# Attention: two heads per stack in the array's row halves, exponentials two banks wide, maxima issued in pairs, V kept in SBUF

## The chip, the cores and the metric

One of the eight cores of a Trainium2 chip runs the whole program. The metric is the device time of one execution in microseconds; the time before is the median of three runs.

## The reference, cut to what matters

Two layers; only the first attention is touched. Its weights and inputs are float32 (2 batches, 1024 tokens, 256 features, 16 heads).

```python
qkv = layernorm(x) @ W_attn                  # q1 k1 q2 k2 (128 columns each), v (256)
attn1 = q1 @ k1.T * hd**-0.5                 # per head, hd = 8
attn2 = q2 @ k2.T * hd**-0.5
score = softmax(attn1 - lam * attn2)         # 1024 x 1024 per head, 16 heads, 2 batches
x = x + ((1 - LAMBDA_INIT) * (score @ v)) @ W_proj
```

After it come a ternary feed-forward layer, a linear attention with 32 heads and a routed layer.

## The kernel before, in words

Instructions are placed by hand: each engine runs its own list in order and waits on semaphores. Six stages follow each other; between two of them all engines meet, and a stage may start only when every engine has reached its end.

`stage_qkv` (L157) normalizes x in four chunks of 512 tokens, transposes them and multiplies by W_attn. Every product is made of a rounded high part and the low rest, three matmuls each. With the scale and lambda folded into Q, one head is 16 rows of Q and 16 of K, and the score is one product. SyncE (L213 to L245) stores high and low parts of Q and K of each chunk to DRAM (L233) and then the chunk's V (four stores, L237), whose rows are padded to 32 columns a head, with a one in column 16. V waits for ScalarE's eviction (L366). After chunk 1 SyncE issues the loads of the first stack. The stage ends for SyncE when that stack has landed (L245). POOL (L248) fills the padding: two V buffers and, by `pad` (L430), the rows of two stacks that no load writes; VectorE meanwhile normalizes chunk 0 (L114, L123, L141) and scales the row of factors (L316, L317), for which TensorE waits at L385.

`stage_attention` (L440) works on groups of four heads, eight groups over both batches. A **stack** (`qst`, `kst`, three of each in turn) holds the four heads one behind the other: on 128 partitions, of which 50 carry data: Q high, Q low, Q high against K high, K high, K low, and two rows of minus the maximum (high and low) against ones. `load_stack` (L417) fills it with seven DMAs. For each group:

- **Maxima** (L572): 64 matmuls 128x512, queries on the partitions, go to three PSUM banks `ps_m` in turn; VectorE reduces each (L710). Then `finish_max` makes the row of 4096 maxima, and SyncE writes it into the stack with eight small DMAs (L535).
- **Scores** (L592): 64 matmuls 128x512, keys on the partitions, into three banks `ps_s`; the two extra rows subtract the maximum. ScalarE exponentiates each (L684) into `prob`.
- **Values** (L605): for every 128 keys and 512 queries one value unit, four heads side by side in four strips of 32 columns of the array, in float32 (two instructions a matmul), summed over the eight key tiles in one of two `ps_o` banks. The one in V's column 16 gives the sum of the exponentials.
- **Out**: ScalarE copies the bank (L691), TensorE transposes it (L578) through `ps_m`, VectorE divides (L720 to L723).

The order on TensorE is written out. Score units are numbered u; a unit is one head and 128 keys and has two score matmuls. `side` gives the maxima and transposes that stand beside unit u; the maxima of group g+1 start six units ahead of group g, two a unit; value units follow at u % 4 = 1 and 3:

```python
side[max(-1, UPG * (g - 1) - LEAD + m // MPU)].append(("max", g, m))
```

`side[-1]` holds what runs before the first score: all 64 maxima of group 0 and 12 of group 1. The ternary weights of the next stage are made beside them (ScalarE L660 to L675, POOL L546 to L554, transposes L631 between the maxima), in the memory of `prob`. `pe.wait_ge(m_rd, n - BANKS + 1)` lets maximum n start when the third before it is reduced; `pe.wait_ge(exp_ok, n - BANKS + 1)` does the same for scores.

Of the kernel before, what the change touches and what calls it, by code (L numbers as in the profile page):

```python
# [22 lines left out]
P = 128  # L23
# [133 lines left out]
def stage_qkv(nc, d, io, keep, scratch):  # L157


    with ExitStack() as ctx:  # L160
        st = Store(nc, ctx, "qkv")
        X, ident, qst = keep["X"], keep["ident"], keep["qst"]
        q_dram, v_dram, zero_dram = scratch["qk"], scratch["v"], scratch["zero"]
# [6 lines left out]
        qk_lo = st.sb("qk_lo", [P, 2, NQ, d.CH], F32R)  # L170

        v_st = [st.sb("v_st", [P, d.TPC, d.H, 32])[:],
                keep["tern"][:].rearrange("p a n -> p (a n)").bitcast(F32)
                .rearrange("p (t h c) -> p t h c", t=d.TPC, h=d.H)]
# [3 lines left out]
        VG = d.H // d.G  # L178

# [18 lines left out]
        qk_out, v_out = scratch["qk_out"], scratch["v_out"]  # L198
        v_ps, v_ok, v_init, pad_ok, z_out = (st.sem(n) for n in ("v_ps", "v_ok", "v_init", "pad_ok", "z_out"))
# [12 lines left out]
        with nc.Block() as block:  # L212
            @block.sync  # L213
            def _(sp):
# [10 lines left out]
                sp.wait_ge(pad_ok, 1)  # L225
                sp.dma_start(zero_dram, as_f32(qst[0][64:66]).rearrange("r h t -> r (h t)")).then_inc(z_out, 16)
                for c in range(d.NC):
# [7 lines left out]
                    sp.wait_ge(v_ok, 2 * (c + 1))  # L235
                    for g in range(VG):
                        sp.dma_start(v_dram[b, g, :, t0 // P:t0 // P + d.TPC, :],  # L237
                                     v_st[c % 2][:, :, d.G * g:d.G * (g + 1), :].rearrange("p t h c -> p t (h c)"))\
                            .then_inc(v_out[c % 2], 16)
                    if c == d.S // d.CH - 1:  # L240
                        sp.wait_ge(z_out, 16)
# [6 lines left out]
            def _(pool):  # L248
# [80 lines left out]
            def _(act):  # L329
# [17 lines left out]
                for c in range(d.NC):  # L347
# [12 lines left out]
                    for j in range(2):  # L360
                        act.wait_ge(v_ps, 2 * c + j + 1)
                        if c < 2:
                            act.wait_ge(v_init, c + 1)
                        else:
                            act.wait_ge(v_out[c % 2], 16 * VG * (c // 2))
                        nc.scalar.activation(v_st[c % 2][:, 2 * j:2 * j + 2, :, 0:d.HD],  # L366
# [47 lines left out]
STACK_LOADS = 7  # L414


def load_stack(d, keep, scratch, g, sp, sem):  # L417
# [3 lines left out]
    for base, dst, parts in ((0, qst, (0, 1, 0)), (d.E, kst, (0, 0, 1))):  # L421
        for n, part in enumerate(parts):
            src = scratch["qk"][part, b, base + h0 * d.HD:base + (h0 + d.G) * d.HD, :]
            sp.dma_start(as_f32(dst[n * d.HD:(n + 1) * d.HD, :, :]),
                         src.rearrange("(h e) t -> e h t", e=d.HD)).then_inc(sem, 16)
    sp.dma_start(as_f32(qst[3 * d.HD:3 * d.HD + 2, :, :]), scratch["zero"].rearrange("r (h t) -> r h t", h=d.G))\
        .then_inc(sem, 16)


def pad(nc, link, keep, i):  # L430

    qst, kst = keep["qst"][i], keep["kst"][i]
    link(nc.gpsimd.memset(as_f32(qst[64:P, :, :]), 0.0))
    link(nc.gpsimd.memset(as_f32(kst[64:P, :, :]), 0.0))
    link(nc.gpsimd.memset(as_f32(qst[32:64, :, :]), 0.0))
    return nc.gpsimd.memset(as_f32(kst[32:64, :, :]), 1.0)

# [1779 lines left out]
```

## Time and profile before

| what | us |
|---|---|
| median of three runs (lowest, highest) | 1344.59 (1342.28, 1345.54) |
| span of the profiled execution | 1344.7 |
| its TensorE, busy | 1139.2 (85%) |
| its VectorE, busy | 921.8 (69%) |
| its ScalarE, busy | 630.1 (47%) |
| its POOL, busy | 231.4 (17%) |
| mean granted clock of TensorE | 0.911 |

Busy time is the time in which an engine had at least one instruction in work, over the whole program. TensorE's matmuls overlap, so what one costs in a row of them is the distance between their starts, not its duration. "PEld" is TensorE's weight load, which runs beside the matmul before. A granted clock of 1.00 is 2.4 GHz, 0.50 is 1.2 GHz. "SPq" is SyncE's queue, which issues the DMAs. "Idle before" is the engine's idle time ahead of an instruction, with what ended it.

### The profile page before, as it was taken

The page shows a single profiled execution, that of the slowest core. Times are in us where ns is not written, and L with a number is a line of the kernel's source. Part 1 is how long each engine was busy: PE and PEld are TensorE (multiplying, and loading weights), DVE is VectorE, ACT ScalarE, POOL GpSimd, SP SyncE. Part 2 cuts the span into 40 slices and gives each one's busy share as a digit, 9 for nine tenths or more (in the row PEclk, how much of TensorE's full clock was granted, in tenths as well). Part 3 has the DMA queues.
Part 4 walks back from the last instruction along what each step waited for, and adds up shares of the span by engine and source line. Part 5 has one row for each costly group of instructions (what it writes and reads, how often), then busy time and mean ns, then how long its engine had stood idle before and what let it go on. Part 6 is the DMA issues. An engine that isn't in the chain of part 4 may idle for free. (4 is left out here: it accounts for less than half of the span.)

```text
span 1344.7 us, 16323 instructions
## 1 busy us (share of the span) xinstructions
PE 1139.2 (85%) x5920; PEld 820.3 (61%) x5920; DVE 921.8 (69%) x1953; ACT 630.1 (47%) x1106; POOL 231.4 (17%) x178
## 2 busy tenths in 40 slices
PE   0959999999999998655575747999999799999888
PEld 0834555555555533544464635888887589889786
DVE  8739888888888820458988867555554677777743
ACT  2413766676666676267664213333333433433233
POOL 9006300000000000100003322100000644744200
PEclk9965999999999999777787878999999899999859
DMA  2794422421431000000000020100000000000200
GB/s 87 213 287 66 65 33 34 64 41 26 64 39 28 1 2 32 4 1 0 1 1 1 1 82 1 48 17 32 33 16 0 32 1 1 1 1 1 83 0 4
DMA packets 34221, 48.55 MB, mean 36 GB/s; under 512 B 5310, under 2 KB 22218, under 8 KB 34122
## 3 DMA queue, kind: packets, MB, share of 16 engines
q1 hardware_dynamic: 34140, 47.51, 16.0%
q8 instruction: 47, 0.77, 0.2%
q14 instruction: 34, 0.28, 0.1%
HBM read 32.52 MB, written 14.71 MB: 35 GB/s over the span
## 5 line engine op out<-in xcount | busy, mean ns | idle before, releaser
L710 DVE TENSOR_REDUCE att_mx<-att_ps_m 128x1 f32<-128x512 f32 x512 | 316.3, 681 | 66.8 <-PE att_ps_m L572 66.8
L684 ACT ACTIVATE att_prob<-att_ps_s 128x512 f32<-128x512 f32 x512 | 267.2, 604 | 115.6 <-PE att_ps_s L592 115.5
L572 PE MATMUL att_ps_m<-kst,qst 128*128 128x512 f32 x512 | 227.5, 468 | 18.5 <-PEq L74 16.0
L592 PE MATMUL att_ps_s<-qst,kst 128*128 128x512 f32 x512 | 200.7, 404 | 4.9 <-ACT att_prob L684 4.7
L572 PEld LDWEIGHTS att_ps_m<-kst,qst 128*128 128x128 f32 x512 | 102.3, 200 | 142.2 <-DVE att_mx L710 111.0
L1719 POOL TENSOR_TENSOR qry_prod<-qry_qr,lin_ksum 128x512 f32<-128x512 f32 x64 | 87.9, 1375 | 307.3 <-ACT qry_qr L1786 307.3
L605 PE MATMUL att_ps_o<-att_prob,att_vst 128*32 128x512 f32 x1024 | 136.2, 604 | 0.0
L592 PEld LDWEIGHTS att_ps_s<-qst,kst 128*128 128x128 f32 x512 | 94.8, 188 | 42.3 <-ACT att_prob L684 27.8
L1786 ACT ACTIVATE qry_qr<-qry_ps_q 128x512 f32<-128x512 f32 x64 | 38.3, 598 | 129.8 <-PE qry_ps_q L152 116.4
L1462 DVE SCALAR_TENSOR_TENSOR key_k_lo<-key_ps_k,key_k_hi 128x512 fp32r<-128x512 f32 x64 | 44.2, 690 | 67.8 <-ACT key_k_hi L1542 67.3
L1103 ACT ACTIVATE mlp_junk<-mlp_z,mlp_nlev 128x1024 bf16<-128x1024 f32 x64 | 72.6, 1137 | 23.2 <-DVE mlp_nlev L939 21.6
L152 PE MATMUL qry_ps_o<-qry_m_hi,qry_n_hi 128*128 128x256 f32 x256 | 76.5, 299 | 0.9 <-DVE qry_n_lo L1749 0.8
L152 PE MATMUL qry_ps_o<-qry_m_lo,qry_n_hi 128*128 128x256 f32 x256 | 71.0, 277 | 0.0
L152 PE MATMUL qry_ps_o<-qry_m_hi,qry_n_lo 128*128 128x256 f32 x256 | 70.9, 277 | 0.0
L1749 DVE TENSOR_TENSOR qry_n_lo<-qry_ps_t,qry_n_hi 128x512 fp32r<-128x512 f32 x64 | 44.2, 691 | 37.3 <-ACT qry_n_hi L1775 36.9
L1542 ACT ACTIVATE key_k_hi<-key_ps_k 128x512 fp32r<-128x512 f32 x64 | 38.2, 597 | 66.0 <-PE key_ps_k L152 65.3
L829 POOL CAST mlp_wo_t<-ternary 128x2048 f32<-128x2048 bf16 x1 | 1.9, 1891 | 386.4 <-POOLq L508 386.4
L152 PE MATMUL key_ps_k<-key_w_hi,lin_xt_hi 128*128 128x512 f32 x128 | 54.2, 424 | 1.7 <-DVE lin_xt_lo L1421 1.7
L1739 DVE SCALAR_TENSOR_TENSOR qry_qn<-qry_rec,qry_qr 128x512 f32<-128x512 f32 x64 | 53.5, 836 | 2.2
L152 PE MATMUL qry_ps_q<-qry_w_hi,lin_xt_hi 128*128 128x512 f32 x128 | 51.7, 404 | 3.3 <-DVE qry_w_lo L1759 3.3
L152 PE MATMUL qry_ps_q<-qry_w_lo,lin_xt_hi 128*128 128x512 f32 x128 | 51.5, 402 | 0.0
L152 PE MATMUL key_ps_g<-key_k_hi,key_xk_hi 128*128 128x512 f32 x128 | 50.5, 395 | 0.6 <-DVE key_k_lo L1462 0.6
(348 smaller groups left out, 2395.6 us busy)
## 6 DMA issues: line engine op xcount, KB each, us to landing
qst<-qk_parts SPq DMA_DIRECT2D x24, 256.0 KB
kst<-qk_parts SPq DMA_DIRECT2D x24, 256.0 KB
qk_parts<-att_out SPq DMA_DIRECT2D x16, 256.0 KB, 3.3
qk_parts<-qkv_qk_lo SPq DMA_DIRECT2D x16, 256.0 KB, 3.4
att_vst<-v_rows SPq DMA_DIRECT2D x8, 512.0 KB
residual<-L_attn_x SPq DMA_DIRECT2D x4, 512.0 KB, 5.7
v_rows<-qkv_v_st SPq DMA_DIRECT2D x8, 256.0 KB, 5.4
v_rows<-ternary SPq DMA_DIRECT2D x8, 256.0 KB, 4.0
```

Of the source, the lines that this page charges most:

```text
L152: ins = nc.tensor.matmul(out, a, b, start=first and n == 0, stop=last and n == len(terms) - 1)
L572: nc.tensor.matmul(ps_m[:, n % BANKS, :], qst[g % RING][:, h, t * P:(t + 1) * P], kst[g % RING][:, h, half * d.CH:(half + 1) * d.CH], star ...
L592: nc.tensor.matmul(ps_s[:, n % BANKS, :], kst[g % RING][:, h, s * P:(s + 1) * P], qst[g % RING][:, h, t * d.CH:(t + 1) * d.CH], start=True ...
L605: ins = nc.tensor.matmul(ps_o[32 * h:32 * h + 32, t, :], vst[g % RING][:, s, 32 * h:32 * h + 32], prob[:, n % RING, h, t * d.CH:(t + 1) * ...
L684: nc.scalar.activation(prob[:, s % RING, h, t * d.CH:(t + 1) * d.CH], ps_s[:, n % BANKS, :], ACT.Exp).then_inc(exp_ok, 1)
L710: nc.vector.reduce_max(mx[:, g % 2, m // NB, m % NB:m % NB + 1], ps_m[:, n % BANKS, :], AX.X)\
L1103: nc.scalar.activation(junk[:, n % 2, :], Z[:, t, :], ACT.Sign, bias=nlev[:, t:t + 1], accum_out=sgn[:, t:t + 1]).then_inc(cnt_ok, 1)
L1462: nc.vector.scalar_tensor_tensor(out=k_lo[:, i % 2, :], in0=ps_k[:, i % 2, :], scalar=0.0, in1=as_f32(k_hi[:, i % 2, :]), op0=ALU.max, op1 ...
L1719: nc.gpsimd.tensor_tensor(prod[:, u % 2, :], qr[:, u % 2, :], ksum[:, b, cols(n)], ALU.mult).then_inc(pr_ok, 1)
L1739: nc.vector.scalar_tensor_tensor(out=qn[:, u % 2, :].rearrange("p (h e) -> p h e", e=HW), in0=rec[:].unsqueeze(2).to_broadcast([P, HPB, HW ...
L1749: nc.vector.tensor_tensor(n_lo[:, u % 2, :], ps_t[:, u % 2, :], as_f32(n_hi[:, u % 2, :]), ALU.subtract).then_inc(n_ok, 1)
L1786: nc.scalar.activation(qr[:, u % 2, :], ps_q[:, u % 2, :], ACT.Relu).then_inc(q_ok, 1)
```

## The change

A stack now has two heads above each other: rows 0 to 49 hold heads 0 and 2 of the group, rows 64 to 113 (`ROW2` = 64) heads 1 and 3, one pair behind the other. Matmuls take 48 or 50 rows of one half, so two of them (a pair) address the two halves of the array's rows and write two banks. Score pairs have two times two banks, and one exponential reads two banks (1024 columns). Max pairs use three banks `ps_m`, maxima stay 512 columns each. `ps_o` is one bank. A step u is now 128 keys, 512 queries and four heads: two score pairs, two max pairs, and the value work of an earlier step (`LAG`), cut in two halves of 256 queries, except for the first key tile. The order of loops becomes group, query half, key tile. V stays in SBUF (`vall`), so its stores and loads and the zero rows go. A stack is loaded with 12 DMAs, a row of maxima written with 16. POOL fills `vall` and 32 rows of each half of `kst`; nothing is filled in the attention stage.

```diff
@@ stage_qkv: SyncE @@
-                sp.wait_ge(pad_ok, 1)
-                sp.dma_start(zero_dram, as_f32(qst[0][64:66]).rearrange("r h t -> r (h t)")).then_inc(z_out, 16)
...
-                    sp.wait_ge(v_ok, 2 * (c + 1))
-                    for g in range(VG):
-                        sp.dma_start(v_dram[b, g, :, t0 // P:t0 // P + d.TPC, :],
...
@@ stage_qkv: POOL @@
-                for i in range(2):
-                    link(nc.gpsimd.memset(v_st[i], 0.0))
-                    nc.gpsimd.memset(v_st[i][:, :, :, d.HD:d.HD + 1], 1.0).then_inc(v_init, 1)
-                    pool.wait_ge(v_init, i + 1)
-                for i in range(len(qst) - 1):
-                    pad(nc, link, keep, i).then_inc(pad_ok, 1)
+                link(nc.gpsimd.memset(vall[:], 0.0))
+                nc.gpsimd.memset(vall[:, :, :, d.HD:d.HD + 1], 1.0).then_inc(v_init, 1)
+                pool.wait_ge(v_init, 1)
+                for i in range(2 * len(kst)):
+                    rows = slice(ROW2 * (i % 2) + 32, ROW2 * (i % 2) + 64)
+                    nc.gpsimd.memset(as_f32(kst[i // 2][rows, :, :]), 1.0).then_inc(pad_ok, 1)
                     pool.wait_ge(pad_ok, i + 1)
@@ load_stack @@
-            sp.dma_start(as_f32(dst[n * d.HD:(n + 1) * d.HD, :, :]),
-                         src.rearrange("(h e) t -> e h t", e=d.HD)).then_inc(sem, 16)
...
+            for r in range(2):
+                row = ROW2 * r + n * d.HD
+                sp.dma_start(as_f32(dst[row:row + d.HD, :, :]), src[r]).then_inc(sem, 16)
@@ stage_attention: sizes and order @@
-        LEAD = 6
-        SUM_AT, TURN_AT = 34, (64, 71)
+        PR = 6
+        LEAD = 5
+        LAG = 2
+        HALF = d.CH // 2
+        SUM_AT, TURN_AT = 17, (32, 37)
...
+        SPG = NS * NB
+        MPG = PAIRS * NS * NB
+        STEPS = SPG * d.NG
+        NMD = 16
...
+                side[max(-1, SPG * (g - 1) - LEAD + m // PAIRS)].append(("max", g, m))
             for t in range(NB):
+                side[NS * (NB * g + t + 1) + LAG + 2].append(("out", g, t))
...
+        for u in range(STEPS):
+            for c in range(2):
+                slot = 2 * (u + LAG) + c
+                if u % NS < 2:
+                    slot = 2 * (u // NS * NS + LAG + 1) + u % NS
+                values.setdefault(slot, []).append((u, c))
@@ stage_attention: TensorE @@
                     if kind == "max":
+                        if n + 1 >= MB:
+                            pe.wait_ge(m_rd, n + 2 - MB)
...
+                        for r in range(2):
+                            rows = slice(ROW2 * r, ROW2 * r + 3 * HD)
+                            ins = nc.tensor.matmul(ps_m[:, (n + r) % MB, :], qst[g % RING][rows, j, t * P:(t + 1) * P],
+                                                   kst[g % RING][rows, j, half * d.CH:(half + 1) * d.CH],
+                                                   start=True, stop=True)
+                        ins.then_inc(m_ps, 2)
...
+                def score_pair(u, j):
...
+                        pe.wait_ge(exp_ok, p - 1)
+                    for r in range(2):
+                        rows = slice(ROW2 * r, ROW2 * r + 3 * HD + 2)
+                        ins = nc.tensor.matmul(ps_s[:, 2 * (p % 2) + r, :], kst[g % RING][rows, j, s * P:(s + 1) * P],
+                                               qst[g % RING][rows, j, t * d.CH:(t + 1) * d.CH], start=True, stop=True)
+                    ins.then_inc(sc_ps, 1)
+
+                def value_half(u, c):
...
+                    cols = slice(c * HALF, (c + 1) * HALF) if s else slice(0, d.CH)
                     for h in range(G):
+                        ins = nc.tensor.matmul(ps_o[32 * h:32 * h + 32, cols], vall[:, NS * b + s, h0 + h, :],
+                                               prob[:, u % PR, h, cols], start=s == 0,
+                                               stop=s == NS - 1 and c == 1)
...
+                for u in range(END):
                     todo = side[u]
+                    for j in range(PAIRS):
+                        if u < STEPS:
+                            score_pair(u, j)
                         for x in todo[:1]:
                             side_unit(*x)
                         todo = todo[1:]
+                        for v in values.get(2 * u + j, []):
+                            value_half(*v)
                     for x in todo:
                         side_unit(*x)
@@ stage_attention: ScalarE @@
+                        nc.scalar.activation(prob[:, u % PR, 2 * j:2 * j + 2, :],
+                                             ps_s[:, 2 * (p % 2):2 * (p % 2) + 2, :], ACT.Exp).then_inc(exp_ok, 1)
@@ stage_attention: VectorE @@
+                        dve.wait_ge(m_ps, n + 2)
+                        for r in range(2):
+                            nc.vector.reduce_max(mx[:, g % 2, r, m:m + 1], ps_m[:, (n + r) % MB, :], AX.X)\
+                                .then_inc(m_rd, 1)
```

## Rows read from the trace of the kernel before

**Rows 1.** The stages' windows: us, busy us (instructions) by engine, PEclk, DMA share, GB/s

```profile
0.00:89.70 89.70, 41.13 (x226) 35.95 (x227) 56.32 (x115) 25.92 (x46) 32.92 (x19) 0.93 0.64 186
89.70:139.00 49.30, 46.54 (x112) 25.05 (x112) 48.34 (x80) 16.58 (x18) 27.51 (x9) 0.60 0.51 108
139.00:477.50 338.50, 337.77 (x1776) 175.24 (x1776) 284.09 (x498) 233.15 (x449) 7.14 (x3) 1.00 0.29 39
477.50:531.00 53.50, 48.80 (x262) 17.69 (x259) 2.83 (x12) 41.41 (x80) 0.00 (x0) 1.00 0.01 1
531.00:1344.70 813.70, 664.99 (x3552) 566.39 (x3550) 530.26 (x1251) 313.03 (x514) 163.79 (x149) 0.88 0.05 16
```

**Rows 2.** Waits of 139 to 477 us: waited for, us in total, times, longest

```profile
ACT att_prob L684 <- PE att_ps_s L592: 105.2, 112, 1.4
```

**Rows 3.** Timeline of one period of the main part: start, us, engine, line

```profile
172.30 0.39 PE L572 MATMUL att_ps_m<-kst,qst 128*128 128x512 f32 x1
...
172.53 0.39 PE L592 MATMUL att_ps_s<-qst,kst 128*128 128x512 f32 x1
...
172.84 0.16 PEld L605 LDWEIGHTS att_ps_o<-att_prob,att_vst 128*32 128x32 f32 x8 [0.35 <-ACT att_prob L684]
172.84 1.06 PE L605 MATMUL att_ps_o<-att_prob,att_vst 128*32 128x512 f32 x8
...
173.84 0.50 PE L572 MATMUL att_ps_m<-kst,qst 128*128 128x512 f32 x1
...
174.18 0.39 PE L592 MATMUL att_ps_s<-qst,kst 128*128 128x512 f32 x1
...
174.38 2.48 DVE L710 TENSOR_REDUCE att_mx<-att_ps_m 128x1 f32<-128x512 f32 x4 [0.55 <-PE att_ps_m L572]
```

**Rows 4.** Timeline of the first 36 us: VectorE, POOL, TensorE

```profile
5.78 3.51 POOL L433 MEMSET qst<- 64x4096 f32 x1
...
6.73 2.58 DVE L114 TENSOR_SCALAR qkv_ve<-qkv_mv 128x4 f32<-128x4 f32 x1
...
13.11 14.24 DVE L141 TENSOR_SCALAR qkv_xn<-residual,qkv_mv,qkv_rstd 128x256 f32<-128x256 f32 x4
...
32.41 2.00 DVE L316 TENSOR_SCALAR qkv_row<-qkv_row,qkv_lam 1x64 f32<-1x64 f32 x1
...
34.49 0.58 PE L385 MATMUL qkv_ps_v<-qkv_one,qkv_row 1*128 1x1 f32 x2 [5.06 <-DVE qkv_row L317]
```

**Rows 5.** Timeline around the gap before attention

```profile
67.22 12.30 SPq L237 DMA_DIRECT2D v_rows<-qkv_v_st  x4
...
73.72 0.60 ACT L366 ACTIVATE ternary<-qkv_ps_v 128x512 f32<-128x512 f32 x1 [0.83 <-PE qkv_ps_v L152]
...
85.66 3.19 SPq L237 DMA_DIRECT2D v_rows<-ternary  x4
...
89.69 0.93 PEld L572 LDWEIGHTS att_ps_m<-kst,qst 128*128 128x128 f32 x3 [16.21 <-issue]
```

**Rows 6.** One window inside that gap

```profile
76.00:78.00 2.00, 0.00 (x0) 0.00 (x0) 0.00 (x0) 0.00 (x0) 0.00 (x0) 0.94 1.06 394
```

**Rows 7.** Timeline of attention's opening

```profile
90.52 38.39 DVE L710 TENSOR_REDUCE att_mx<-att_ps_m 128x1 f32<-128x512 f32 x64 [18.35 <-PE att_ps_m L572]
...
91.27 0.29 PEld L572 LDWEIGHTS att_ps_m<-kst,qst 128*128 128x128 f32 x1 [0.65 <-DVE att_mx L710]
...
132.25 2.52 SPq L535 DMA_DIRECT2D qst<-att_nm_hi  x4
```

**Rows 8.** Groups of instructions, shapes apart: busy us, mean ns, idle before

```profile
L684 ACT ACTIVATE att_prob<-att_ps_s 128x512 f32<-128x512 f32 x512 | 267.2, 604 | 115.6 <-PE att_ps_s L592 115.5
...
L660 ACT ACTIVATE att_prob<-att_prob 128x2048 f32<-128x2048 f32 x2 | 3.8, 1911 | 27.7 <-DMA att_prob<-L_ffn_W_syn 25.3 <-DMA att_prob<-L_ffn_W_out 2.4
...
L2123 PE MATMUL rt_ps_a<-rt_h,rt_gate 128*8 128x256 f32 x32 | 7.4, 379 | 0.0
...
L605 PE MATMUL att_ps_o<-att_prob,att_vst 128*32 128x512 f32 x1024 | 136.2, 604 | 0.0
```

More of the change, by code:

```diff
@@ L446, in stage_attention @@
         st = Store(nc, ctx, "att")
-        AO, ident, qst, kst, tern, sc = (keep[n] for n in ("AO", "ident", "qst", "kst", "tern", "sc"))
+        AO, ident, qst, kst, tern, sc, vall = (keep[n] for n in ("AO", "ident", "qst", "kst", "tern", "sc", "v"))
         NS = d.S // P
@@ L483, in stage_attention, with place @@
         TB = d.KT * d.N // d.CH
-        UPG = NS * G
-        MPG = G * NS * NB
-        MPU = MPG // UPG
-        UN = UPG * d.NG
-        LOADS = STACK_LOADS + 1
-        NMD = 8
-        side = {u: [] for u in range(-1, UN + 2 * G + 3)}
+        SPG = NS * NB
+        MPG = PAIRS * NS * NB
+        STEPS = SPG * d.NG
+        NMD = 16
+        END = STEPS + LAG + 4
+        side = {u: [] for u in range(-1, END)}
         for g in range(d.NG):
             for m in range(MPG):
-                side[max(-1, UPG * (g - 1) - LEAD + m // MPU)].append(("max", g, m))
+                side[max(-1, SPG * (g - 1) - LEAD + m // PAIRS)].append(("max", g, m))
             for t in range(NB):
-                side[UPG * (g + 1) + G + 2 + t].append(("out", g, t))
-        items = [(u, x) for u in side for x in side[u]]
+                side[NS * (NB * g + t + 1) + LAG + 2].append(("out", g, t))
+        items = [x for u in side for x in side[u]]
+        first, total = {}, 0
+        for x in items:
+            first[x] = total
+            total += 2 if x[0] == "max" else 1
+        values = {}
+        for u in range(STEPS):
[4 more added lines that the diff above has]
+                values.setdefault(slot, []).append((u, c))
         def loaded(g):
-            return 16 * (LOADS * (g // RING + 1) - (STACK_LOADS if g % RING == 0 else 0))
-        def ready(kind, g, m):
-            return [x for _, x in items].index((kind, g, m)) + 1
+            return 16 * STACK_LOADS * (g // RING + (0 if g % RING == 0 else 1))
+        def place(kind, g, m):
+            return first[kind, g, m] + 1
         with nc.Block() as block:
@@ L556, in _ @@
                     pool.wait_ge(tern_ok, i + 1)
-                pad(nc, link, keep, RING - 1).then_inc(pad_ok, 1)
             @block.tensor
             def _(pe):
-                done = [0]
                 def side_unit(kind, g, m):
-                    n = done[0]
-                    done[0] += 1
-                    if n >= BANKS:
-                        pe.wait_ge(m_rd, n - BANKS + 1)
+                    n = first[kind, g, m]
                     if kind == "max":
-                        h, t, half = m // (NS * NB), m // NB % NS, m % NB
+                        if n + 1 >= MB:
+                            pe.wait_ge(m_rd, n + 2 - MB)
+                        j, t, half = m // (NS * NB), m // NB % NS, m % NB
@@ L570, in side_unit @@
                         if m == 0 and g:
                             pe.wait_ge(load[g % RING], loaded(g))
-                        nc.tensor.matmul(ps_m[:, n % BANKS, :], qst[g % RING][:, h, t * P:(t + 1) * P],
-                                         kst[g % RING][:, h, half * d.CH:(half + 1) * d.CH],
-                                         start=True, stop=True).then_inc(m_ps, 1)
+                        for r in range(2):
[3 more added lines that the diff above has]
+                                                   start=True, stop=True)
@@ L638, in _ @@
                         prologue[TURN_AT[i] + k] = lambda i=i, k=k: turn_weight(i, k)
-                for n, x in enumerate(side.pop(-1)):
+                for n, x in enumerate(side[-1]):
                     side_unit(*x)
```

174 lines of the change are left out of this document (70 added, 104 removed).

## The prediction

> **What bounds the kernel now.** I read the windows by stage first: the scaled input projection and everything ahead of the attention stage take 89.7 us, the attention stage's opening (maxima of the first head group alone, weights made ternary) 49.3, its main part 338.5, its tail without maxima 53.5, and the rest of the program 813.7, which the change does not touch [rows 1]. In the main part TensorE is busy throughout, at full granted clock; VectorE 84%, ScalarE 69%. The waits there say the same: ScalarE waits 105.2 us of it for scores [rows 2]. One period of the timeline shows why TensorE binds: matmuls of 512 columns follow each other every 0.23 us, eight of them (four maxima, four scores), then 0.08 us to get into the value unit, 1.00 us for its eight instructions, and about 0.11 us to get out, which is 3.03 us; VectorE's four maxima fill 2.48 of it [rows 3]. 338.5 us hold 109 such periods (436 maxima), so 3.10 each with the transposes.
>
> **The front: POOL's fills.** POOL and VectorE share something here: L114's 4-element tensor_scalar, asked for at 6.73, lasts until 9.31, just behind POOL's fill of 5.78 to 9.29; the four L141 last 14.24 us, one fill each; L316 waits until 34.4 for the last fill; TensorE's L385 starts at 34.49 [rows 4]. The change replaces eight fills of 4096 elements per partition (3.51 each) and two of 2048 by one of 8192 (7.0), a small one (0.2 to 0.4) and six of 2048 on 32 partitions (half of 3.51, 1.76, plus 0.06 between). So POOL is done at about 20 instead of 34.4. VectorE: L114 ends with the large fill at 8.6, L123, three short steps later, with the first of the six at 10.8, the four L141 with a fill each: 12.6, 14.4, 16.3, 18.1, where they ended at 27.35. Gain so far 9.2. L316 came 5.1 after them, now at 23.2, when POOL is idle, and with L317 takes some 0.3 instead of 2.0: L385 at 23.5. **Gain 11.0**; bounds 9 (L316's part lost) and 12.
>
> **The gap before attention.** The last projection result leaves ScalarE at 74.3 and the first weight load of a maximum starts at 89.69. Between them SyncE is stuck in stores of V: the third chunk's four issues take 12.30 us from 67.22, the fourth's end at 88.85 [rows 5], and at 76 to 78 the DMA engines are still full, at 394 GB/s [rows 6]. With V kept in SBUF all 16 stores and 8 loads of V go, the stores of chunk 3's Q and K are issued as they are computed, and the stack (same bytes in 12 issues instead of 7, plus some 2 us of SyncE, hidden) should land by then, since it was issued ahead of all that. The stage then ends with ScalarE at 74.3 plus the 0.84 that 88.85 to 89.69 shows: 75.2. **Gain 14.4**; bounds 9 (the queue still holds SyncE up for 5 us) and 15.
>
> **The opening: costlier.** Here VectorE is the bound now, 64 maxima in 38.39 us, 0.60 each, with three banks [rows 7]. The change issues them in pairs into the same three banks, so that a pair may start only when one maximum of the pair before is left. VectorE frees a bank 0.75 us after it starts a maximum (90.52 to 91.27), and from a weight load to the maximum behind it takes 0.83 at the clock granted here (89.69 to 90.52; the clock falls during TensorE's pause, its mean is 0.94 at 76 to 78 and 0.60 over the opening [rows 1, 6]). If the two halves run side by side, a pair repeats every 0.75 + 0.83 + 0.01 = 1.59 us, not 1.20. 42 pairs (32 of group 0, 10 of group 1) stand before the first score; I take the last eight at full clock (1.28, below), since the transposes of the ternary weights stand between them and fill TensorE: 0.8 + 34 x 1.59 + 8 x 1.28 = 65 us instead of 49.3. The row of maxima goes out in 16 DMAs instead of 8, each 0.63 of SyncE [rows 7]: 10 us where 5 were; they start at about 53 of the 65 us and land at 64, just hidden. **Loss 15.8**. The ternary work runs beside it.
>
> **The main part.** I call half a step a slot: a score pair, a max pair, half a value unit. TensorE: weight load 0.11 (0.34 after a value unit less 0.23), two pair streams 0.46, 0.09 into value mode, the half unit. That form is in no row: it costs between 0.50 and 1.00. float32 instructions of 256 and 512 columns last 379 and 604 ns [rows 8], 0.225 apart, and two stand behind each other, so 1.00 - 0.45 = 0.55 to 0.57. I take 0.57: slot 1.23. VectorE: 0.75 until the bank is free, 0.54 from weight load to maximum at full clock (173.84 to 174.38): 1.28 per pair against 1.20 of work. ScalarE: 512 columns 0.604, 2048 columns 1.91 [rows 8], so 0.85 ns a column; 1024 take about 1.04, or 0.95 repeating. So VectorE, slowed by its three banks, sets the slot at 1.28. Eight steps (16 slots) are a round: 14 intervals of 1.28; one of 1.65, where TensorE has the undivided first value unit between two max pairs (0.11 + 0.23 + 0.09 + 1.00 + 0.22); and one of 3.3, with two value halves together (1.1), two score pairs (0.67), a max pair (0.23), four transposes (0.7) and another half (0.6). Sum 22.9 a round, against 8 x 3.10 = 24.8. 214 pairs are left, 13.4 rounds: 306 us instead of 338.5. **Gain 32.5**. The maxima's DMAs (2.7 us until issue, 9.5 of issues, 1.8 landing) have about 17 us here, so they stay covered.
>
> **The tail.** 21 steps have no maxima: a slot is 0.11 + 0.23 + 0.09 + 0.57 = 1.00 on TensorE, 0.95 on ScalarE; with the undivided units and transposes 17.5 a round, 46 in all, and 3.5 to finish, against 53.5. **Gain 4.**
>
> **Sum:** 1344.7 - 11.0 - 14.4 + 15.8 - 32.5 - 4.0 = 1298.6. The profiled execution spans 1344.7 us, the median of the runs is 1344.59, so nothing is to be corrected: 1299.
>
> **The pair's price.** Two halves of the rows at once stand in no row; the nearest is the value unit, where eight matmuls of 0.6 us in four column strips take 1.00 us together [rows 3]. A pair costs between one stream (0.23) and two (0.46). I take the first, by that row. The Trainium skill's TensorE: Matmul & The Clock Gate, section Part 3: Packing small matmuls, gives 3.07 times for four row tiles where four would be ideal; by that share a pair would be 0.30, 0.07 more, and my sum about 1322. No row here shows it.
>
> **Rivals.**
> *Weight loads queue.* If the two halves' weight loads follow each other (0.11 each; double at half clock), every pair is late by one: 34 x 0.21 + 8 x 0.11 + 214 x 0.11 + 42 x 0.11 = 36 us more: 1334. Against it: the value unit's eight loads take 0.16 us together. With partial overlap of the streams this case covers 1315 to 1340. Chance 0.18.
> *Slower: the halves run one after the other.* Pairs take 0.46: TensorE's slot is 0.11 + 0.92 + 0.09 + 0.57 = 1.69, and TensorE binds. Against the forecast: 34 x 0.43 + 8 x 0.23 in the opening (16), 0.41 x 14 + 1.1 a round (92), 0.23 x 42 in the tail (10): 1417. It decides from about 0.1 us of extra time per pair, some two fifths of a stream. Nothing in the trace excludes it; the strips speak against. Chance 0.10.
> *The clock.* TensorE would stream 0.89 of each 1.42 us, less than before, and in the opening much less. The tail (66% streaming, clock 1.00 [rows 1]) speaks against a fall in the main part. At clock 0.50 a slot is about 2.15 and a round 38.5; three such rounds of 13.4 undo the gain. Chance 0.06, two thirds of it slower. The other way: the shorter pause (1.7 us) leaves the clock up in the opening: pairs of 1.28, 10.5 us less, 1288. Chance 0.10.
> *Nothing gained inside attention* (PE's issue or semaphores fill what pairing frees), only front and gap: about 1335 to 1345. Chance 0.04, half of it no change.
>
> **Numbers.** The forecast has 0.52. Range 1280 (clock up in the opening, tail 5 better) to 1340. Within 0.3% (4 us, about what a measurement of this kernel can tell from no change) is 0.03, slower 0.14, faster 0.83.
>
> **What would show it.** L385 near 24 and the first maximum at about 64; the maximum's repeat 1.6 us per pair in the opening, 1.28 later; first score at about 129 and last maximum at about 435; VectorE waiting some 0.08 us per pair for TensorE. Wrong if row halves start 0.2 us apart, if granted clock falls after 130, or if scores wait for qst's maxima DMAs.

## The result and the profile after

The changed kernel takes 1327.5 us (median of 4 runs, 1320.2 to 1329.9) against 1343.7 (4 runs, 1342.3 to 1345.5): ratio 0.9862, interval 0.9831 to 0.9893. It is 16 us faster where 45 were forecast. The profiled execution took 1327.15 us and spans 1325.3, 26.7 more than the forecast sum of 1298.6. Of all the runs below one is left out of its median, g3's of 1323.6 us, which ran at a mean clock of 0.894 where g3's other three have 0.91 to 0.92. The windows below are the stages as the prediction cut them [rows 1]: projection, opening, main part, tail, rest of the program; columns as there.

```profile
0.00:63.60 63.60, 40.21 (x226) 35.21 (x227) 45.70 (x115) 25.90 (x46) 19.11 (x15) 1.00 0.58 171
63.60:130.60 67.00, 41.18 (x118) 18.10 (x118) 53.53 (x86) 16.52 (x18) 20.54 (x7) 0.51 0.39 95
130.60:455.60 325.00, 298.19 (x2472) 116.84 (x2474) 291.14 (x490) 224.22 (x229) 0.00 (x0) 0.93 0.21 29
455.60:514.00 58.40, 52.36 (x458) 18.51 (x450) 3.38 (x13) 42.64 (x45) 0.00 (x0) 0.85 0.01 2
514.00:1325.30 811.30, 666.44 (x3548) 567.22 (x3548) 529.85 (x1249) 312.79 (x514) 163.74 (x149) 0.89 0.05 16
```

Look at the granted clock: 0.93 in the main part and 0.85 in the tail, where before it was 1.00 in both. The opening is at 0.51, half clock throughout.

**Front and gap.** The timeline of the first 25 us, and what answers to [rows 4] in it; the last line, from the timeline of the weight loads, answers to [rows 5]:

```profile
1.53 6.92 POOL L243 MEMSET v_rows<- 128x8192 f32 x1
6.79 1.69 DVE L114 TENSOR_SCALAR qkv_ve<-qkv_mv 128x4 f32<-128x4 f32 x1
9.10 11.22 POOL L248 MEMSET kst<- 32x2048 f32 x6
11.16 7.42 DVE L141 TENSOR_SCALAR qkv_xn<-residual,qkv_mv,qkv_rstd 128x256 f32<-128x256 f32 x4
24.03 0.58 PE L372 MATMUL qkv_ps_v<-qkv_one,qkv_row 1*128 1x1 f32 x2 [3.37 <-DVE qkv_row L305]
...
63.60 0.21 PEld L558 LDWEIGHTS att_ps_m<-kst,qst 48*128 48x128 f32 x2 [1.50 <-issue]
```

VectorE's short instruction still ends with POOL's large fill (8.48 and 8.45), and the four L141 take 7.42 us instead of 14.24, beside POOL's shorter fills. POOL is done at 20.3, TensorE goes on at 24.03 instead of 34.49. The first maximum is at 63.60 instead of 89.69: 10.5 us of that are the front's, 15.6 the gap's.

**A full-clock slot.** The timeline of the main part around 262 us:

```profile
262.17 0.39 PE L582 MATMUL att_ps_s<-qst,kst 50*128 50x512 f32 x2
263.11 0.19 PEld L558 LDWEIGHTS att_ps_m<-kst,qst 48*128 48x128 f32 x2 [0.98 <-DVE att_mx L705]
263.12 0.49 PE L558 MATMUL att_ps_m<-kst,qst 48*128 48x512 f32 x2 [0.56 <-DVE att_mx L705]
...
264.40 0.50 PE L558 MATMUL att_ps_m<-kst,qst 48*128 48x512 f32 x2 [0.56 <-DVE att_mx L705]
```

The two matmuls of a pair stand in one row (x2): together they last 0.50 us, no more than one of them did before (0.39 to 0.50 [rows 3]). So the halves run side by side. What a pair costs in a row of them is the distance between starts; no pairs stand back to back here, but they do in f5 (below), whose filling pairs go to two banks and therefore have a row for each half:

```profile
76.37 0.39 PE L639 MATMUL att_ps_o<-kst,qst 48*128 48x512 f32 x1
76.37 0.39 PE L639 MATMUL att_ps_s<-kst,qst 48*128 48x512 f32 x1
76.60 0.39 PE L639 MATMUL att_ps_o<-kst,qst 48*128 48x512 f32 x1
76.61 0.39 PE L639 MATMUL att_ps_s<-kst,qst 48*128 48x512 f32 x1
```

A pair every 0.23 us is one stream's price. From one max pair to the next in the changed kernel it is 264.40 - 263.12 = 1.28 us, set by VectorE with three banks; TensorE idles 0.56 of it ahead of each of these two max pairs, because no value unit stands there. These two neighbouring idle pieces come once a round, and a single one of 0.55 us some 8 us behind them.

**The rounds.** Here is the main part cut at ScalarE's copies of the value bank (L683), one every eight steps, so that each window holds 32 maxima and the same matmuls (x188 of PE in each):

```profile
164.60:188.10 23.50, 21.35 (x188) 8.54 (x188) 22.22 (x40) 16.70 (x19) 0.00 (x0) 1.00 0.35 48
188.10:211.00 22.90, 21.07 (x188) 8.46 (x188) 21.39 (x36) 16.62 (x19) 0.00 (x0) 1.00 0.18 23
211.00:241.00 30.00, 28.17 (x188) 9.74 (x188) 22.14 (x40) 16.60 (x18) 0.00 (x0) 0.72 0.36 49
241.00:264.00 23.00, 21.03 (x188) 8.46 (x188) 21.49 (x36) 16.72 (x19) 0.00 (x0) 1.00 0.06 9
264.00:287.40 23.40, 21.34 (x188) 8.54 (x188) 22.12 (x40) 16.63 (x19) 0.00 (x0) 1.00 0.35 49
287.40:310.30 22.90, 21.07 (x188) 8.46 (x188) 21.39 (x36) 16.61 (x18) 0.00 (x0) 1.00 0.18 23
310.30:334.80 24.50, 22.56 (x188) 8.72 (x188) 22.22 (x40) 16.73 (x19) 0.00 (x0) 0.93 0.33 47
334.80:357.70 22.90, 21.08 (x188) 8.47 (x188) 21.39 (x36) 16.60 (x18) 0.00 (x0) 1.00 0.19 23
357.70:382.20 24.50, 22.62 (x188) 8.76 (x188) 22.15 (x40) 16.63 (x18) 0.00 (x0) 0.93 0.33 46
382.20:408.20 26.00, 24.13 (x188) 9.33 (x188) 21.45 (x36) 16.66 (x18) 0.00 (x0) 0.87 0.16 20
408.20:431.60 23.40, 21.32 (x188) 8.54 (x188) 22.12 (x40) 16.64 (x18) 0.00 (x0) 1.00 0.02 3
431.60:454.60 23.00, 21.06 (x188) 8.46 (x188) 21.49 (x36) 16.70 (x19) 0.00 (x0) 1.00 0.00 1
```

This table holds most of the answer. A round at full clock takes 22.9 us, as forecast, or 23.4 when VectorE also gathers a group's maxima (x40 of VectorE instead of x36). The four rounds with the clock below 1.00 (five falls, two of them in the round of 30.0) took 6.6, 1.1, 1.1 and 3.1 more than their like: 11.9 us. DMA shows no such link: at 0.35 one round took 23.4.

### The profile page after: what moved, and what is told of

The parts are those of the page before. It is cut to its first block and busy times, and to the rows that moved or that the text cites. A ratio compares the mean times of both kernels' runs of the same rounds, so it can differ in the third digit from the quotient of the medians.

```text
span 1325.3 us, 18000 instructions
## 1 busy us (share of the span) xinstructions
PE 1098.4 (83%) x6816; PEld 755.9 (57%) x6816; DVE 923.6 (70%) x1953; ACT 622.1 (47%) x850; POOL 203.4 (15%) x170
## 5 line engine op out<-in xcount | busy, mean ns | idle before, releaser
L705 DVE TENSOR_REDUCE att_mx<-att_ps_m 128x1 f32<-128x512 f32 x512 | 329.3, 685 | 37.5 <-PE att_ps_m L558 37.2
L675 ACT ACTIVATE att_prob<-att_ps_s 128x1024 f32<-128x1024 f32 x256 | 259.6, 1025 | 114.4 <-PE att_ps_s L582 114.0
L558 PE MATMUL att_ps_m<-kst,qst 48*128 48x512 f32 x512 | 135.7, 526 | 53.0 <-DVE att_mx L705 51.7
L598 PE MATMUL att_ps_o<-att_prob,v_rows 128*32 128x256 f32 (+1 forms) x1920 | 169.0, 434 | 2.6 <-ACT att_osb L683 2.6
L582 PE MATMUL att_ps_s<-qst,kst 50*128 50x512 f32 x512 | 131.4, 510 | 3.6 <-DMA qst<-att_nm_lo 2.1
L558 PEld LDWEIGHTS att_ps_m<-kst,qst 48*128 48x128 f32 x512 | 54.4, 209 | 112.5 <-DVE att_mx L705 98.1
L582 PEld LDWEIGHTS att_ps_s<-qst,kst 50*128 50x128 f32 x512 | 50.9, 196 | 107.8 <-issue 72.0
L598 PEld LDWEIGHTS att_ps_o<-att_prob,v_rows 128*32 128x32 f32 x1920 | 41.2, 112 | 68.6 <-issue 61.7
```

Source lines behind the costliest of these rows:

```text
L558: ins = nc.tensor.matmul(ps_m[:, (n + r) % MB, :], qst[g % RING][rows, j, t * P:(t + 1) * P], kst[g % RING][rows, j, half * d.CH:(half + 1 ...
L582: ins = nc.tensor.matmul(ps_s[:, 2 * (p % 2) + r, :], kst[g % RING][rows, j, s * P:(s + 1) * P], qst[g % RING][rows, j, t * d.CH:(t + 1) * ...
L598: ins = nc.tensor.matmul(ps_o[32 * h:32 * h + 32, cols], vall[:, NS * b + s, h0 + h, :], prob[:, u % PR, h, cols], start=s == 0, stop=s == ...
L675: nc.scalar.activation(prob[:, u % PR, 2 * j:2 * j + 2, :], ps_s[:, 2 * (p % 2):2 * (p % 2) + 2, :], ACT.Exp).then_inc(exp_ok, 1)
L705: nc.vector.reduce_max(mx[:, g % 2, r, m:m + 1], ps_m[:, (n + r) % MB, :], AX.X)\
```

## The experiments

Two theories. **Clock**: what is missing is TensorE at half clock. **Rival**: it is stalls that would be there at any clock (the maxima's transfers, the gathering of a group, banks), and the falls of the clock cost little. All kernels start from the changed one; "profile" is the span of the profiled execution.

### Filling TensorE's idle time in the opening

```
for n, x in enumerate(side[-1]):
    side_unit(*x)
+   for k in range(6):                     # rows 0.. into ps_o, rows 64.. into ps_s[3]; three, all into ps_o, from the 32nd pair on
+       nc.tensor.matmul(<bank>, qst[0][rows, 0, 0:P], kst[0][rows, 0, 0:d.CH], start=True, stop=True)
```

> The changed kernel with idle time of TensorE in the opening filled: behind each pair of maxima of the first group, six more matmuls of the same shape go into banks that nobody reads. Clock theory (the missing gain is TensorE at half clock): the granted clock comes back to 1.00 soon after the first maxima, a pair repeats every 1.28 us instead of 1.59, the opening lasts 54 to 57 us instead of 67.0, the first 17 us of the main part run at full clock too and give 3 more, so about 1311 to 1315 against the 1327.5 of the changed kernel. Rival (the pair repeat is set by VectorE and the three banks whatever the clock is): the opening stays at 67 and the time at 1327, or grows with the fillers to 1340. The main part after 30 us of it and the tail stay as they are under both.

1326.3 us (1325.3 to 1328.8), no gain. Yet the first part did what the clock theory says; two windows, and the timeline where they meet:

```profile
64.40:107.00 42.60, 39.67 (x261) 22.71 (x262) 41.76 (x67) 11.68 (x9) 18.64 (x7) 1.00 0.53 146
107.00:133.90 26.90, 24.48 (x76) 15.48 (x77) 13.81 (x21) 4.94 (x9) 2.04 (x1) 0.52 0.45 60
```

```profile
99.82 9.22 POOL L543 TENSOR_TENSOR att_prob<-att_prob 128x2048 f32<-128x2048 f32 x2
...
106.84 2.24 DVE L704 CAST att_nm_hi<-att_nmt 128x32 fp32r<-128x32 f32 x1
...
109.96 0.80 PE L559 MATMUL att_ps_m<-kst,qst 48*128 48x512 f32 x2 [2.42 <-DVE att_mx L713]
```

At full clock the pair repeats in 1.28 us and VectorE is 98% busy. Then VectorE's small copy, 0.18 us in other groups, lasts 2.24, to the end of POOL's subtraction; TensorE stands 2.42 us, and after that the matmul is at half clock (0.80 us). The fillers behind it, now slower (the 26.9 us window has clock 0.52), gave the gain back. So the opening has a second bound, POOL's work on the ternary weights.

### Filling the empty slots of the main part, and its control

Per eight steps two slots have no value unit. e2 issues the score pair twice there; f6 issues the same number of extra pairs in a step with two value halves. The two idle pieces stand half a slot later than the two doubled pairs, so in e2 only the first of them gets shorter:

```profile
258.24 0.50 PE L559 MATMUL att_ps_m<-kst,qst 48*128 48x512 f32 x2 [0.33 <-DVE att_mx L707]
...
259.53 0.50 PE L559 MATMUL att_ps_m<-kst,qst 48*128 48x512 f32 x2 [0.56 <-DVE att_mx L707]
```

Where this document and the expectations speak of filled slots, this is what was filled: 0.55 and 0.55 us became 0.33 and 0.56.

```
-for r in range(2):
+for k in range(2 if 2 * u + j in values else 4):      # f6: 4 if u % NS == 5 else 2
+    r = k % 2
     rows = slice(ROW2 * r, ROW2 * r + 3 * HD + 2)
     ins = nc.tensor.matmul(ps_s[:, 2 * (p % 2) + r, :], ...)
```

> The changed kernel with each score pair issued twice in the slots that have no value unit (two per eight steps, where TensorE idles 0.55 us twice, just ahead of most falls of the clock). Clock theory: these dips bring the granted clock down; filled, the falls in the main part (at 213, 223, 313, 360 and 382 us) are gone or fewer, which gives back up to 13 us of the main part: 1314 to 1320. Rival (the falls follow the maxima's last steps of a group, or come by chance): as many falls as before, 1327, and 0.2 us more per dip at worst, 1331.

> Control of e2: the same number of extra score pairs, two per eight steps, but in the step with two half value units, not in the empty slots. If what brings the clock down is the quiet stretch around the empty slots: the falls of the main part stay as in the changed kernel, and the extra pairs cost about 0.2 us each: 1330 to 1335. If it is TensorE's mean activity: the falls go as they did in e2, 1314 to 1320.

e2: 1316.3 us (1312.8 to 1329.5), ratio 0.9819 (0.9764 to 0.9874). The windows of its opening, main part and tail:

```profile
64.00:131.10 67.10, 41.19 (x118) 18.14 (x118) 53.53 (x86) 16.51 (x18) 20.56 (x7) 0.52 0.38 101
131.10:446.90 315.80, 293.03 (x2536) 122.01 (x2538) 291.07 (x490) 224.37 (x229) 0.00 (x0) 0.97 0.19 30
446.90:499.90 53.00, 47.90 (x462) 17.66 (x461) 3.45 (x14) 42.66 (x45) 0.00 (x0) 0.97 0.01 2
```

TensorE does more (x2536 for x2472), and main part and tail are 9 and 5 us shorter; against the second profiled execution of the changed kernel (f8 below: 321.3 and 57.9) it is 5.5 and 5. By the medians e2 gains 7 to 11 us (1323.6 and 1327.5 are the changed kernel's two medians). f6: 1323.0 (1319.3 to 1325.1), between its two expectations and no gain over the 1323.6 that the changed kernel took on the same chip; its profile has two falls in the main part where the changed kernel's has five.

What the profiles add, and what the expectations did not single out, is where the falls begin. In the five with these slots untouched and `LEAD` 5 (changed, f8, e1, f7, e4), 22 of the 23 falls in the rounds of the main part begin within 0.9 us behind the second of the two neighbouring idle pieces, and both of f6's do; the other, at 222.3 us of the changed kernel, follows the single piece by 1.8 us. In f6 TensorE's idle time in the rounds sums to 20.6 us, in e2 to 21.1, in the changed kernel to 23.2. So the sum of idle time doesn't tell e2 from f6; the neighbouring pieces do, which f6 leaves as they were. One profiled execution of each is little to go by, though, and e2's slowest run (1329.5, mean clock 0.885 where its profiled one had 0.900) shows that the falls become rarer, not impossible.

### The maxima one step further ahead

`LEAD = 6` instead of 5; g4 is that with e2's doubled scores.

> The changed kernel with the maxima one step further ahead of their scores (LEAD 6 instead of 5). At 466.4 us the first score of the last group waits 2.06 us for the maxima's transfers and the clock falls just behind it. If that wait is what brings the tail down to half clock: the wait is gone, the tail stays at 1.00 and lasts 50 us or less instead of 57.6; the opening gets two pairs longer (3.2 us) and the main part shorter by as much: about 1320. If the tail falls by itself, because it has no maxima and TensorE does less: the wait is gone, the fall stays, 1325 to 1327.

> LEAD 6 as in e3, with the doubled score pairs of e2. e3 was 10 us slower than the changed kernel, and its rounds of eight steps took 22.95 to 27.96 us with the clock falling once in most of them. If the falls are the whole of that: filled, the rounds are 23.1 to 23.7, main part and opening together 382 to 385 (e2: 382.2), and the time is that of e2, 1311 to 1317. If LEAD 6 has a cost of its own (a wait for a stack or for the maxima's buffers): rounds stay above 24 at full clock, 1325 to 1335.

e3: 1337.3 (1331.7 to 1339.3), 10 us slower, which neither side expected. The wait for the maxima's transfers ahead of the last group is gone, and still the tail has clock 0.91 (0.85 before) and lasts 56.7 us: that wait was not all that brings it down. The main part fell to 0.90. Its timeline shows why: the gathering of a group now comes right ahead of the empty slots, and TensorE idles 1.41 us in one piece where the longest in the changed kernel's rounds is 0.56; one max pair later it runs at half clock (0.80). Six such pieces of 1.40 us stand in its main part, and behind each the clock falls within 2.4 us.

```profile
215.90 0.39 PE L582 MATMUL att_ps_s<-qst,kst 50*128 50x512 f32 x2
217.70 0.64 PE L558 MATMUL att_ps_m<-kst,qst 48*128 48x512 f32 x2 [1.41 <-DVE att_mx L705]
...
219.12 0.80 PE L558 MATMUL att_ps_m<-kst,qst 48*128 48x512 f32 x2 [0.36 <-DVE att_mx L705]
```

g4: 1327.3 (1324.2 to 1329.2), a miss for the number: the doubled scores leave 1.01 us of that idle time, and its clock in the window of the table below is 0.95. Its undisturbed rounds take 23.1, as in e2, so LEAD 6 has no cost of its own at full clock.

### The stores of V put back

```
+sp.wait_ge(v_ok, 2 * (c + 1))
+for g in range(VG):
+    sp.dma_start(v_dram[b, g, :, t0 // P:t0 // P + d.TPC, :], <vall of chunk c>).then_inc(v_out[c % 2], 16)
# and, in the attention stage, SyncE waits for v_out ahead of the weights' loads
```

> The changed kernel with the 16 stores of V to DRAM put back in SyncE's queue of the projection stage, which nobody reads any more. If the gap ahead of attention (15.6 us of the gain measured) was SyncE held up by these stores: the first maximum starts at 76 to 79 us instead of 63.6 and the time is about 1340 to 1343. If it was something else that the change took away (the zero rows, the seventh load, the V loads behind them): the first maximum stays below 68 and the time at 1327 to 1331.

1337.3 us (2 runs), 3 below the expectation. SyncE's issues and the first maximum's weight load:

```profile
59.34 8.23 SPq L231 DMA_DIRECT2D v_spill<-v_rows  x3
...
77.67 0.32 PEld L565 LDWEIGHTS att_ps_m<-kst,qst 48*128 48x128 f32 x2 [15.15 <-issue]
```

The first maximum moves from 63.6 to 77.7, by 14.1 of the gap's 15.6 us: the gap was, all but 1.5 us, these stores in SyncE's queue. The time rose by less, 9.7 us against 1327.5 and 13.7 against the 1323.6 of f8, because main part and tail took 321.3 and 57.9 us, as in f8.

### A fourth bank for the opening's maxima

```
-ps_m = st.ps("ps_m", [P, MB, d.CH]);      ps_o = st.ps("ps_o", [P, d.CH])
+ps_m = st.ps("ps_m", [P, MB + 1, d.CH]);  ps_o = ps_m[:, MB, :]
+# maxima ahead of the first score: bank n % 4, wait for m_rd >= n - 2; behind it n % 3 as before
```

> The changed kernel with a fourth bank for the maxima of the opening (the value bank, not needed there yet). The prediction read the opening's pair as 0.75 until VectorE frees a bank plus 0.83 until the next maximum starts at half clock, because pairs share three banks. By that a pair repeats in VectorE's own 1.20 to 1.23 us although TensorE stays at half clock, the first group's maxima are done some 11 us earlier, and the opening is 56 to 62 us instead of 67.0 (ternary weights and the maxima's transfers become the bound): 1316 to 1322. Rival (half clock itself makes TensorE too slow for VectorE): the repeat stays near 1.6 and the time at 1327.

1308.6 us (1306.7 to 1312.2), ratio 0.9723 (0.9698 to 0.9748). Weight loads in its opening, and those of the changed kernel below:

```profile
75.12 0.29 PEld L565 LDWEIGHTS att_ps_m<-kst,qst 48*128 48x128 f32 x2 [0.90 <-DVE att_mx L712]
76.31 0.29 PEld L565 LDWEIGHTS att_ps_m<-kst,qst 48*128 48x128 f32 x2 [0.91 <-DVE att_mx L712]
77.51 0.29 PEld L565 LDWEIGHTS att_ps_m<-kst,qst 48*128 48x128 f32 x2 [0.91 <-DVE att_mx L712]
```

```profile
75.71 0.29 PEld L558 LDWEIGHTS att_ps_m<-kst,qst 48*128 48x128 f32 x2 [1.29 <-DVE att_mx L705]
77.29 0.29 PEld L558 LDWEIGHTS att_ps_m<-kst,qst 48*128 48x128 f32 x2 [1.30 <-DVE att_mx L705]
```

Both are at half clock (0.29 us a load); the repeat is 1.20 with four banks and 1.58 with three. The opening is 55.7 us instead of 67.0; that is 11.3 of the 14.9 us by which its profiled execution is shorter (1310.4). The main part gives 5.7 more (319.3 us at clock 0.95, for 325.0 at 0.93), the tail 0.6, and what follows attention was 2.7 longer. So the mechanism gives the 11, and it went below the 1316 expected by fewer falls of the clock, as the changed kernel itself does in its better runs. The forecast's reading of the opening, banks times half clock, holds to 0.01 us.

### The changed kernel again, and combinations

> The changed kernel as it is, for the spread of its runs against their mean granted clock. Clock theory: its runs differ by where the clock falls, so time and mean clock go together, about 0.4 us of time per us spent at half clock. Rival (the spread has another cause): times of 1320 to 1330 at the same mean clock.

1323.6 us median (1315.1 to 1324.3). The nine runs of the changed kernel span mean clocks from 0.880 (1329.9 us) to 0.893 (1315.1). With 2 x (1 - clock) x span as the time at half clock, these two are at 318.7 and 281.1 us: 14.8 us of time for 37.6 of half clock, 0.39 each, and a straight line through all nine gives the same 0.39 (correlation 0.99). The spread of the runs goes with the clock's. The five falls in the rounds of the changed kernel's profile give the same price: 11.9 us lost in 30.7 at half clock.

f5 has both fillers, the weights' sum five pairs earlier and the weight transposes two later; g1 the four banks, e2's doubled scores and the sum two pairs earlier; g2 is g1 with the scores three times; g3 is g1 with fillers in the opening and at its two waits, and the weight transposes two pairs later.

> The changed kernel with both fillers, the scores issued twice in the slots without a value unit and six filling matmuls behind each pair of the opening (while a score bank is free for them), and with the weights' sum put behind the 13th pair of maxima instead of the 18th and the weight transposes behind the 35th instead of the 33rd, so that POOL is done before VectorE gathers the first group's maxima (in e1 POOL's subtraction stretched VectorE's copy from 0.18 to 2.24 us, TensorE stood 2.4 us, and the clock fell). Clock theory: opening 55 to 60 us instead of 67.0, no half clock at the start of the main part (3 more), main part 312, tail 53 as in e2: 1311.0 of e2's profiled run less 10 to 14, about 1299 to 1304 for a run like it. Rival (something else holds the opening: the maxima's transfers or the ternary work): opening 64 to 67, 1308 to 1316.

> The four banks of the opening (f7) together with the doubled score pairs in the empty slots (e2), and the weights' sum behind the 16th pair instead of the 18th, as late as the weights themselves allow. If the two gains are what the traces say, they add: f7's profiled 1310.4, less some 5 to 6 for the falls in its main part, less 4 to 5 for the half clock in its tail, less 2 for POOL being done earlier: about 1298 to 1301. If the doubled pairs only moved the falls about by chance (e2's slowest run took 1329.5 us): 1306 to 1310.

> As g1, but the scores of the empty slots issued three times instead of twice, which fills 0.46 of the 0.55 us of idle time. Clock theory: as fast as g1 or up to 3 us slower in its profiled run, with less spread between its runs, since no run falls in the main part; rival (the score's delay of 0.46 us reaches ScalarE or VectorE): rounds of 23.6 us and more instead of 23.14, 3 to 8 us slower than g1 in all runs.

> As g1 with four filling matmuls behind each pair of the opening into two score banks, and sixteen of them at each of two waits (VectorE gathering the first maxima, the transfers of the maxima ahead of the first score), so that the clock is at 1.00 when the scores start. Clock theory: no half clock in the first 16 us of the main part, 3 us less than g1, 1295 to 1298. Rival (the fillers themselves hold up what follows, by up to 3.7 us each): 1300 to 1304.

The main part from the first copy of the value bank to the last maximum, the same work in each but for the extra pairs (and one pair of maxima or two less in e3 and g4), by the windows view:

| kernel | median us (runs) | profile, us | this window, us | granted clock |
|---|---|---|---|---|
| changed | 1327.5 (4) | 1325.3 | 290.3 | 0.95 |
| f8, changed again | 1323.6 (5) | 1321.8 | 286.8 | 0.96 |
| e1 | 1326.3 (4) | 1324.2 | 285.6 | 0.97 |
| f7, four banks | 1308.6 (4) | 1310.4 | 285.7 | 0.97 |
| e2, empty slots filled | 1316.3 (4) | 1311.0 | 280.6 | 1.00 |
| f5 | 1315.4 (4) | 1308.2 | 280.7 | 1.00 |
| g1, f7 with e2 | 1305.3 (6) | 1303.4 | 280.7 | 1.00 |
| g3 | 1304.7 (3) | 1302.8 | 280.6 | 1.00 |
| g2, scores three times | 1310.7 (5) | 1308.8 | 289.0 | 0.98 |
| f6, control | 1323.0 (4) | 1319.9 | 284.5 | 0.98 |
| e3, LEAD 6 | 1337.3 (6) | 1334.8 | 299.8 | 0.91 |
| g4, LEAD 6 with e2 | 1327.3 (4) | 1326.5 | 290.8 | 0.95 |
| e4, V's stores back | 1337.3 (2) | 1336.4 | 286.7 | 0.96 |

The four kernels with doubled scores and `LEAD` 5 are at 1.00 and within 0.1 us of each other; none of the seven without reached 1.00, and of the six with extra score pairs in the empty slots g2 and g4 did not either. **f5** missed its 1299 to 1304: the sum now came before the weights were there, TensorE waited for them at 81 us, and the clock fell there and again at 113 us, where its fillers had stopped and TensorE idled 0.94 and 0.79 us (opening 63.0 us). **g1**, at 1305.3 us (1301.1 to 1312.2), ratio 0.9701 (0.9676 to 0.9727), is 18 to 22 us below the changed kernel. g3, at 1304.7 (1302.8 to 1311.6), can't be told from it, and the lead of both over f7 is smaller than their spread. g1 missed its 1298 to 1301 mostly by the tail (56.6 us, e2's 53.0), which fell to half clock again:

```profile
64.20:118.90 54.70, 39.87 (x118) 17.89 (x119) 50.84 (x86) 16.55 (x18) 20.56 (x7) 0.52 0.40 119
118.90:434.20 315.30, 292.50 (x2534) 121.68 (x2536) 291.20 (x490) 224.11 (x229) 0.00 (x0) 0.97 0.21 31
434.20:490.80 56.60, 51.75 (x462) 18.83 (x462) 3.51 (x14) 42.76 (x45) 0.00 (x0) 0.88 0.01 2
```

**g2** idles 0.09 us, not 0.33, in the first of the two pieces, but 0.56 still in the second. Its other rounds are 0.24 us longer than g1's, and it has one long fall (28.9 us for that round, clock 0.76), which its clock theory excluded: more filling was no better. **g3** did bring the main part to 1.00 from the start (311.3 us, 4.0 less than g1), but its opening grew by 4.2 with the fillers, so its rival was right: the fillers cost what they give.

## Why the forecast was wrong

The direction was right and the time lies in the range, but the gain is a third of the forecast. By the prediction's steps, in us against its own numbers (what follows attention took 812 us, 2 less than before):

- **Front**, forecast -11.0: -10.5, by the mechanism named. VectorE's instructions end with POOL's fills, and L385 came at 24.03 for "near 24".
- **Gap**, -14.4: -15.6; shown by e4.
- **Opening**, +15.8: +17.7. The pair's 1.59 was 1.58, shown by f7 to be three banks times half clock. The first 34 pairs took 54.0 us, 0.9 less than forecast. Off was that the last eight run at full clock because the transposes fill TensorE: the clock stayed at half, and from 117.62 to the first score at 130.66 they took 1.63 each for 1.28, 2.8 us more. Where a group of transposes stands between two pairs TensorE has no idle time and the pairs are 1.77 apart, so there half clock makes TensorE the bound. The maxima's DMAs were hidden, as forecast: the 16 issues end at 125.3.
- **Main part**, -32.5: -13.6 (324.9 us for 306). The slot (1.28) and the round (22.9) are right. Of the 18.9 missing, 11.9 are the falls of the clock in four rounds, 3.4 the gathering of a group's maxima (0.5 in each of seven groups, left out of the sum), and the remaining 3.6 lie ahead of the first full round, where the clock was at half until 147 us. g3 supports this last part: with the clock up there it gained 4.0 over g1.
- **Tail**, -4.0: +4.4 (57.6 us to the end of ScalarE's last copy, 53.2 before, 49.5 forecast; the window above ends 0.8 later). By the windows e2's tail, with clock 0.97, took 53.0 for 58.4, so about 4 are the clock's, though its wait for transfers was 0.8 shorter too. The rest is waits: the last group's first score stood 2.06 us for the maxima's transfers,

```profile
463.48 3.75 SPq L523 DMA_DIRECT2D qst<-att_nm_lo  x6
...
468.43 0.79 PE L582 MATMUL att_ps_s<-qst,kst 50*128 50x512 f32 x2 [2.06 <-DMA qst<-att_nm_lo]
```

which "about 17 us" of cover was to hide. From the last reduced maximum (455.57) TensorE had work until 466.37, 10.8 us, and the transfers let the score start only after 12.9; the steps without maxima are shorter, so the cover shrank just there. And TensorE waits for ScalarE's copy of the single value bank, 2.6 us in three rounds. After the 2.06 the clock is at half (0.79 us a pair).

Together: some 22 us of the 26.7 are the clock (11.9 and 3.6 in the main part, about 4 in the tail, 2.8 in the opening). The rest is the gathering and the tail's waits, less what gap and the first 34 pairs gained.

**The step that failed** is the clock in the sum: the terms "306 us" and "46 in all" take main part and tail at full clock throughout and put the cost of half clock there at nothing. Measured it was about 19.5 us, and two of the prediction's own signs of being wrong came, the granted clock falling after 130 and a score waiting for the maxima's DMAs. The ground given was "The tail (66% streaming, clock 1.00 [rows 1]) speaks against a fall in the main part", which gave 0.06 to a case that came in both profiled executions of this kernel. Two smaller terms failed beside it: the gathering, left out (3.4), and the cover of the last transfers (2.06 of waiting). The price in that rival was right: in the fall of 223 to 236 us the max pairs' weight loads stand 2.16 us apart, 2.15 forecast:

```profile
225.52 0.34 PEld L558 LDWEIGHTS att_ps_m<-kst,qst 48*128 48x128 f32 x2
...
227.68 0.34 PEld L558 LDWEIGHTS att_ps_m<-kst,qst 48*128 48x128 f32 x2
```

Wrong was to take another instruction mix as evidence: the tail of before streams whole matmuls over the full array, the changed rounds stream pairs over 48 and 50 rows in each half, with value halves and two empty slots between. TensorE was busy 91% of the tail of before (48.80 of 53.50 us [rows 1]) and 92% of a full-clock round (21.07 of 22.90). What differs in the rows are the idle pieces: none longer than 0.3 us in that tail, two of 0.55 close to each other in the rounds. And I took it as all or nothing, three rounds or none, where the outcome was several short falls. The page TensorE: Matmul & The Clock Gate of the Trainium skill describes such a kernel in Part 1, A second HAM failure mode: a matmul kernel that cycles through PSUM banks idles briefly and often, and its clock goes up and down. The trace agrees: the rounds' longest idle piece is 0.56 us and the clock falls all the same. The same page of the Trainium skill, Part 3, Packing small matmuls, which I weighed (3.07 times for four row tiles), led to an estimate of 0.30 us for a pair. The runs show 0.23 for two row halves, so the measurement decides, and that the time came out near that sum's 1322 is luck: it has another reason.

The rivals "weight loads queue" and "halves one after the other" fall with the row of 263.12: both matmuls of a pair within 0.49 us, and their weight loads within 0.19. What stays open: why the clock falls behind some of the neighbouring idle pieces and not behind others like them, why g2 fell once with the first piece at 0.09 us, and why tails of the same instructions ran at 0.97 once (e2, which waited 1.27 us for the transfers) and at 0.88 in g1 (1.61 us). No run closes the second idle piece, so that a kernel without any would hold the clock is not shown.

## What to carry to other kernels

When a change makes TensorE wait for another engine where it was the bound, the granted clock is part of the price: look for slots in which it now idles, and count time at half clock (here 0.39 us lost per us). Repeating a matmul that is there anyway, in slots where TensorE waits, costs little (0.2 us in a round of 23) and can win more (e2: 7 to 11 us by the medians); put it right ahead of the wait itself, since e2's reached only one of two; the same filler in a stage that then stalls elsewhere (e1, g3) gives it back. Before filling, look for the bank or queue that makes TensorE wait: one more bank in the opening was worth more (15 to 19 us by the medians, 11 of it in the opening's own length) than any filler.

## What the runs showed of the hardware

- The clock falls without any long pause: among twelve rounds whose longest idle piece of TensorE was 0.56 us it fell five times, in four of them, and nearly always right behind two such pieces close to each other (22 of 23 falls in five kernels). With 1.40 us in one piece (e3) it fell within 2.4 us behind all six, and in 2.42 us (e1) it fell too. Nine runs of one program differ by 15 us, and time goes with mean clock at a correlation of 0.99.
- A pair of matmuls in the two row halves costs what one costs (0.50 us together, 0.23 from pair to pair), and a pair's two weight loads 0.19 us together, at full clock.
- VectorE's copy of 128x32 elements took 2.24 us instead of 0.18 beside POOL's subtraction of 128x2048 (e1), as its 4-element instruction had beside POOL's fill [rows 4].
